# VectorE makes every seventh source one-hot only up to quad 66 of 196, ScalarE makes the others

## The chip, the cores and the metric

One core of one Trainium2 chip. The metric is device time in microseconds (us) of one execution of the whole program; the median of several runs is compared. Each execution is one launch with all inputs in HBM.

## The reference, cut to what matters

The program runs four graph layers over one graph of 3125 nodes (64 features) and 100000 edges `src -> dst`. Layers 0, 1 and 3 sum neighbours, `segment_sum(h[src], dst)`, and so need only how often each pair (dst, src) occurs: an adjacency matrix of counts. Layer 2 needs each edge for itself, because the message depends on the edge's type:

```python
edge_index = jnp.stack([src, dst])
x = _layernorm(x + _L0_gnn_ref(x, ..., edge_index), axis=-1)      # 2 rounds of segment_sum(h[src], dst)
x = _layernorm(x + _L1_gnn_ref(x, edge_index, ...), axis=-1)      # 1 round
x = _layernorm(x + _L2_gnn_ref(edge_index, edge_type_100, x, ...), axis=-1)  # circular correlation by edge
x = _layernorm(x + _L3_gnn_ref(x, ..., src, dst), axis=-1)        # 1 round
```

The edges come sorted by `dst`. The change lies in the stage that builds the adjacency matrix, before any layer.

## The kernel before

**The whole.** Up to about 215 us the edges are loaded, keys are computed and ranks for a sort are made. From 215 to 637 us the adjacency matrix is counted (the stage of the change). Then layers 0 and 1 run as dense products with that matrix (to about 1110 us), layer 2 gathers rows by indirect DMAs that GpSimd issues (line 1615, in two rounds, to about 3200 us), and layer 3 is again a dense product.

**The counting stage.** The edges are cut into 196 quads (`NQ`) of 4 x 128 edges, a quad into 2 pairs of 2 x 128 edges (392 pairs, numbered n; quad q has the pairs 2q and 2q+1). For each 128 edges TensorE multiplies a source one-hot (128 edges x 125, `oh_src`, the weights) with a destination one-hot (128 edges x columns of a window, `oh_dst`), which counts the edges of each (src, dst) into PSUM. Because the edges are sorted, a pair touches a narrow window of nodes. The window is 12 nodes in the first and second quarter of the pairs, 17 in the third and 20 in the fourth; times 25 blocks this makes 300, 300, 425 and 500 columns. The quarters begin at quads 0, 49, 98 and 147. A second small product (line 768) counts degrees with `oh_blk`.

**Who does what.**
- VectorE, for each pair n in order: at every 14th pair `oh_blk` for 7 quads (line 710); if n is even and n // 2 is in `VECTOR_QUADS`, the quad's source one-hot (`make_sources`, line 698: one comparison of 128 x 500); two `oh_dst` (line 720); then `add_unit` (line 691), which adds the PSUM result of the pair 6 back (`PAST`) into the adjacency matrix in SBUF. In the first quarter one such addition serves two pairs. Every 28 pairs it loads 28 window starts into registers (lines 680 and 681).
- ScalarE, for each quad not in `VECTOR_QUADS`: four `Square` activations (line 659, one per 128 edges, into `sq_src`, two buffers) and one `Relu` over all four (line 671), which writes `oh_src`. It makes the squares of its next quad before the Relu of this one.
- TensorE waits for the sources (`src_made` or `src_made_here`, by who made them), for `dst_made`, and for a free PSUM bank, and tells `counted` after every 4th pair (`BATCH`).
- GpSimd issues 392 indirect DMAs, one per column of sorted records (line 295), from 86 us on; it is tied to nothing in this stage.

**What couples them.** `oh_src` has 6 buffers (`SRC_RING`), so a source can be made once the quad 6 earlier has been counted; `oh_dst` has 7 buffers (`DST_RING`), PSUM has 7 banks for the results. At the end of the stage VectorE, ScalarE, TensorE and SyncE join; GpSimd doesn't take part, it only waits for the join before its next part (line 1427).

`VECTOR_QUADS` (line 75) is 3, 10, 17, ... 192: 28 quads. The loop of ScalarE and the one-hot of VectorE:

```python
mine = [q for q in range(NQ) if q not in VECTOR_QUADS]
...
for i, q in enumerate(mine):
    if i + 1 < len(mine):
        if i >= 1:
            act.wait_ge(src_made.sem, i)
        squares(i + 1)
    if q >= SRC_RING:
        act.wait_ge(counted.sem, batches(2 * (q - SRC_RING) + 2))
    act.wait_ge(src_squared.sem, i + 1)
    nc.scalar.activation(oh_src[q % SRC_RING][:], sq_src[i % 2][:], ACT.Relu, ...)
...
if n % 2 == 0 and n // 2 in VECTOR_QUADS:
    make_sources(n // 2)
```

Of the kernel before, what the change touches and what calls it, by code (L numbers as in the profile page):

```python
# [47 lines left out]
NQ = 2 * QUADS  # L48
# [23 lines left out]
BATCH = 4  # L72
QUARTER_PAIRS = PAIRS // 4
WINDOWS = (12, 12, 17, WIN)
VECTOR_QUADS = frozenset(range(3, NQ, 7))
RUNS = 3
CHUNK = 4 * LO
CHUNKS = -(-NODES // CHUNK)
# [88 lines left out]
def gnn_stack(nc, a, out):  # L167
    ctx = ExitStack()
    with ctx:
# [130 lines left out]
        with sort:  # L300
# [44 lines left out]
            with together() as block:  # L345
                @block.vector
                def _(dve):
                    link = Chain(dve, vec)
                    for t, v in ((src_i, -1), (dst_i, -1), (typ_i, 0), (nat_src_i, -1), (nat_dst_i, -1)):
                        link(nc.vector.memset(t[:], v))  # L350
                    link(nc.vector.memset(empty[:], 0))
                    link(nc.vector.memset(rank[:], float(RUN * 200)))
                    link(nc.vector.memset(ones_f[:], 1.0))
                    link.close()
# [282 lines left out]
        with ExitStack() as t2:  # L637
# [13 lines left out]
            with together() as block:  # L651
                @block.scalar
                def _(act):
                    mine = [q for q in range(NQ) if q not in VECTOR_QUADS]

# [19 lines left out]
                def _(dve):  # L675
# [18 lines left out]
                    def make_sources(q):  # L694

                        if q >= SRC_RING:
                            dve.wait_ge(counted.sem, batches(2 * (q - SRC_RING) + 2))
                        v.tensor_tensor(oh_src[q % SRC_RING][:],
                                        iota[:, 0:LO].rearrange("p (a l) -> p a l", a=1).to_broadcast([P, QUAD, LO]),
                                        nat_lo[:, q * QUAD:(q + 1) * QUAD].rearrange("p (t a) -> p t a", a=1).to_broadcast([P, QUAD, LO]),  # L700
                                        ALU.is_equal).then_inc(src_made_here.sem, 1)

                    units_added = 0
                    for n in range(PAIRS + 1):
                        if n < PAIRS:
                            if n % (2 * STEP) == 0:
                                u = n // (2 * STEP)
                                if u >= 2:
# [5 lines left out]
                                    .to_broadcast([P, STEP * QUAD, BLOCKS]), ALU.is_equal).then_inc(blk_made.sem, 1)  # L714
                            if n % 2 == 0 and n // 2 in VECTOR_QUADS:
                                make_sources(n // 2)
# [28 lines left out]
                def _(pe):  # L745
                    nc.tensor.matmul(psum[0:LO, deg_bank:deg_bank + BUCKETS], zeros[:], zeros[:, 0:BUCKETS],
                                     start=True, stop=False, skip_group_check=True)
                    for n in range(PAIRS):
# [4 lines left out]
                        if n % 2 == 0:  # L753
                            if q in VECTOR_QUADS:
                                pe.wait_ge(src_made_here.sem, sum(k <= q for k in VECTOR_QUADS))
                            else:
                                pe.wait_ge(src_made.sem, sum(k not in VECTOR_QUADS for k in range(q + 1)))
                        unit = UNIT_OF[n]
# [1766 lines left out]
```

## Time and profile before

| | us |
|---|---|
| median of 3 runs | 3346.01 |
| the runs | 3328.13, 3346.01, 3346.45 |
| time of the profiled execution | 3341.13 |
| its span in the profile | 3339.3 |
| counting stage in it | about 215 to 637 |

A busy time is the time in which an engine ran instructions; a wait is put down to what ended it. "Granted clock" is TensorE's clock as a share of full speed. PE is TensorE, PEld its weight loads, DVE VectorE, ACT ScalarE, POOL GpSimd. The page of the profile gives sums over the whole span; the views by stretches, by tile, of waits and of instructions in order of time cut out the counting stage.

### The profile page before, as it was taken

What the parts mean: (1) busy time and instruction counts of PE and PEld (TensorE: products, weight loads), DVE (VectorE), ACT (ScalarE), POOL (GpSimd) and SP (SyncE); (2) the same over time, 40 slices, a digit from 0 to 9 for tenths busy, and PEclk for the clock granted to TensorE, in tenths of its full rate; (3) what the DMA queues carried; (4) which work ended last, traced back from release to release, by engine and by line L of the source; (5) the groups of instructions that cost most, each with busy time, mean ns of one, the idle gap of its engine ahead of it and who ended that gap; (6) DMA issues with size and microseconds to landing.
All of it is one profiled execution on the core that took longest, in us unless ns stands there. A gap on an engine that the chain in (4) does not pass through costs nothing.

```text
span 3339.3 us, 43437 instructions
## 1 busy us (share of the span) xinstructions
PE 2045.3 (61%) x12631; PEld 1588.5 (48%) x12632; DVE 1638.4 (49%) x4094; ACT 1324.1 (40%) x3259; POOL 1987.7 (60%) x2031
## 2 busy tenths in 40 slices
PE   0038878656748586555655555656666666666657
PEld 0027644323324375555655555535555555555544
DVE  7939999744453432222222222345444454444452
ACT  4249876200121074433534334244334353334322
POOL 0777777202212377777777777277777777777700
PEclk9555565667768655555555555578777787777778
DMA  1000000073400132222222222153222323223271
GB/s 37 1 1 2 2 2 2 7 130 62 56 4 2 46 77 55 52 54 52 53 53 53 54 52 49 43 134 84 78 78 79 79 78 78 79 77 78 61 169 38
DMA packets 172646, 183.05 MB, mean 55 GB/s; under 512 B 68506, under 2 KB 145414, under 8 KB 171667
## 3 DMA queue, kind: packets, MB, share of 16 engines
q1 hardware_dynamic: 100801, 99.30, 13.7%
q0 software_dynamic: 64960, 78.47, 9.5%
q10 hardware_dynamic: 6656, 2.40, 0.3%
q8 instruction: 122, 2.00, 0.2%
q14 instruction: 107, 0.88, 0.1%
HBM read 153.41 MB, written 26.60 MB: 54 GB/s over the span
## 4 chain that ended last, share of the span: by engine, by line
POOL 40%; issue 17%; DVE 16%; PE 15%; DMA 5%; ACT 3%; DVEq 1%; SPq 1%; PEldq 0%; ACTq 0%; PEld 0%; POOLq 0%
POOL adj_again_middle L1615 37%; PE psum L1168 4%; DVE adj L691 4%; DVE oh_dst L720 3%; POOL sorted_edges L295 3%; DMA adj_again_middle<-gather_table,gidx_s 3%; PE psum L1735 2%; PE psum L1164 2%; DVE adj_again_middle L1687 2%; DMA sorted_edges<-block_rows,run_rows 2%; ACT sq_src L659 1%; PE psum L1771 1%; PE psum L1406 1%; ACT oh_src L671 1%; DMA l_v<-in_L_gnn_beta 1%
## 5 line engine op out<-in xcount | busy, mean ns | idle before, releaser
L1615 POOL DMA_INDIRECT adj_again_middle<-gather_table,gidx_s x1568 | 1505.4, 960 | 555.3 <-issue 468.4
L1687 DVE TENSOR_TENSOR adj_again_middle<-adj_again_middle,psum 128x256 f32<-128x256 f32 x1176 | 442.1, 417 | 1141.5 <-DMA adj_again_middle<-gather_table,gidx_s 830.6
L1735 PE MATMUL psum<-rel_parts,oh_t 128*128 128x96 bf16 (+1 forms) x4704 | 564.9, 288 | 709.9 <-DVE adj_again_middle L1687 558.5
L1655 ACT ACTIVATE adj_again_middle<-cst,lo_s 128x125 f32<-128x125 f32 x1664 | 527.1, 388 | 1071.8 <-PE psum L1771 1068.2
L1735 PEld LDWEIGHTS psum<-rel_parts,oh_t 128*128 128x128 bf16 x4704 | 415.8, 127 | 828.6 <-issue 581.2
L1771 PE MATMUL psum<-adj_again_middle,oh_s 128*125 x3328 | 739.0, 381 | 23.7 <-issue 16.7
L1771 PEld LDWEIGHTS psum<-adj_again_middle,oh_s 128*125 128x125 f32 x3328 | 662.5, 288 | 48.8 <-issue 42.6
L295 POOL DMA_INDIRECT sorted_edges<-rec,row_i x392 | 393.2, 1003 | 213.2 <-issue 127.1
L766 PE MATMUL psum<-oh_dst,oh_src 128*125 128x300 bf16 (+2 forms) x784 | 337.3, 522 | 73.0 <-DVE oh_dst L720 55.2
L1427 POOL DMA_INDIRECT sorted_edges<-block_rows,run_rows x64 | 86.7, 1355 | 377.9 <-ACT block_rows L1416 266.5
L1659 ACT ACTIVATE oh_s<-adj_again_middle,cst 128x500 f32<-128x500 f32 x416 | 296.1, 712 | 13.6
L766 PEld LDWEIGHTS psum<-oh_dst,oh_src 128*125 128x125 bf16 x784 | 154.9, 198 | 181.0 <-issue 77.2
L659 ACT ACTIVATE sq_src<-cst,x 128x125 bf16<-128x125 f32 x672 | 212.8, 389 | 61.7 <-SPq L221 56.3
L720 DVE TENSOR_SCALAR oh_dst<-iota,x 128x300 bf16<-128x300 int16 (+2 forms) x784 | 219.7, 326 | 2.1 <-PE psum L768 2.1
L1711 DVE TENSOR_TENSOR adj_again_middle<-adj_again_middle 128x256 f32<-128x256 f32 (+1 forms) x392 | 217.2, 554 | 6.8
L1168 PE MATMUL psum<-adj,parts 125*128 125x500 bf16 (+1 forms) x525 | 153.1, 443 | 79.1 <-DVEq L221 79.1
L691 DVE TENSOR_TENSOR adj<-adj,psum 125x300 f32 (+2 forms) x343 | 188.4, 549 | 22.0 <-issue 20.5
L768 PE MATMUL psum<-oh_blk,oh_src 128*125 128x25 bf16 x784 | 172.6, 220 | 0.0
L768 PEld LDWEIGHTS psum<-oh_blk,oh_src 128*125 128x125 bf16 x784 | 169.3, 216 | 0.0
L1679 DVE TENSOR_SCALAR oh_t<-tb,cst 128x512 bf16<-128x512 bf16 x392 | 148.1, 378 | 6.3 <-DMA tb<-sorted_types 6.2
L671 ACT ACTIVATE oh_src<-sq_src,cst 128x500 bf16<-128x500 bf16 x168 | 117.6, 701 | 76.9 <-PE psum L768 76.7
L1168 PEld LDWEIGHTS psum<-adj,parts 125*128 125x128 bf16 x525 | 56.2, 123 | 134.2 <-issue 114.3
(408 smaller groups left out, 1388.8 us busy)
## 6 DMA issues: line engine op xcount, KB each, us to landing
tb<-sorted_types SPq DMA_DIRECT2D x392, 128.0 KB, 3.2
adj_again_middle<-gather_table,gidx_s POOLq DMA_INDIRECT x1568, 2.5
adj_saved<-adj SPq DMA_DIRECT2D x6, 2734.4 KB
adj_again_middle<-adj_saved SPq DMA_DIRECT2D x3, 2734.4 KB
sorted_edges<-rec,row_i POOLq DMA_INDIRECT x392
adj_again_last<-adj_saved SPq DMA_DIRECT2D x2, 2734.4 KB
adj_again_first<-adj_saved SPq DMA_DIRECT2D x1, 2734.4 KB
adj_saved<-adj SPq DMA_DIRECT2D x6, 317.4 KB
```

Of the source, the lines that this page charges most:

```text
L295: nc.gpsimd.indirect_dma_start(rec_d[0], bass.IndirectOffsetOnAxis(ap=row_i[:, c:c + 1], axis=0), rec[:, c, :], None).then_inc(sent.sem, 16)
L691: v.tensor_tensor(to, to, psum[0:LO, pair_bank(u):pair_bank(u) + wide_ * BLOCKS].rearrange("p (n s) -> p s n", s=BLOCKS), ALU.add).then_in ...
L720: ins = v.tensor_scalar(oh_dst[n % DST_RING][:, k, 0:pair_window(n) * BLOCKS], iota16[:, 0:pair_window(n) * BLOCKS], nat_key[:, 2 * n + k: ...
L766: nc.tensor.matmul(psum[0:LO, pair_bank(unit):pair_bank(unit) + wc], of, oh_dst[n % DST_RING][:, k, 0:wc], start=(begins and k == 0), stop ...
L768: mm = nc.tensor.matmul(psum[0:LO, deg_bank + h * BLOCKS:deg_bank + (h + 1) * BLOCKS], of, oh_blk[n // (2 * STEP) % 2][:, n % (2 * STEP) * ...
L1168: nc.tensor.matmul(psum[:, to:to + w], parts12[:, s, :], adj(s, c), start=(s == 0), stop=False, skip_group_check=True)
L1615: nc.gpsimd.indirect_dma_start(gx[g % DEEP][:, k, :], None, table_d[d], bass.IndirectOffsetOnAxis(ap=gidx_s[:, t:t + 1], axis=0),).then_in ...
L1655: sq = nc.scalar.activation(sq_s[:, k, :], iota[:, 0:LO], ACT.Square, bias=lo_s[:, t:t + 1], scale=-1.0)
L1659: nc.scalar.activation(oh_s[g % OH_S][:], sq_s[:], ACT.Relu, bias=one_col, scale=-2.0).then_inc(oh_s_made.sem, 1)
L1687: mul = v.tensor_tensor(part_prod[:, u * SUB:(u + 1) * SUB, s, :].rearrange("p g (a f) -> p g a f", a=2), rows[:, :, s * d // 2:(s + 1) * ...
L1735: mm = nc.tensor.matmul(ps_rel[:, k * RS:k * RS + W], oh_t[g % (AHEAD + 1)][:, (u * SUB + k) * P:(u * SUB + k + 1) * P], rel_parts[:, s, : ...
L1771: mm = nc.tensor.matmul(psum[0:LO, bass.ds((buckets[n] - less) * d, d)], oh_s[j % OH_S][:, k, :], prod[:, bass.ds(tiles[n] * d, d)], start ...
```

## The change

`VECTOR_QUADS` keeps its first 10 members (3, 10, ... 66) and loses the 18 from 73 on (73, 80, ... 192). For those 18 quads VectorE's comparison is gone, and ScalarE makes four squares and a Relu for each. The semaphore counts that TensorE waits for follow from the set. Nothing else changes.

```diff
-VECTOR_QUADS = frozenset(range(3, NQ, 7))
+VECTOR_QUADS = frozenset(range(3, 70, 7))
```

## Rows read from the trace of the kernel before

**Rows 1.** The page: span, and busy time of each engine over it.
```profile
span 3339.3 us, 43437 instructions
PE 2045.3 (61%) x12631; PEld 1588.5 (48%) x12632; DVE 1638.4 (49%) x4094; ACT 1324.1 (40%) x3259; POOL 1987.7 (60%) x2031
```

**Rows 2.** Stretches of the counting stage: busy time (instructions) by engine, clock, DMA.
```profile
215.00:340.40 125.40, 103.91 (x582) 88.10 (x583) 112.28 (x404) 123.29 (x332) 94.06 (x95) 0.57 0.02 2
340.40:389.20 48.80, 41.24 (x206) 31.56 (x204) 46.01 (x159) 42.24 (x112) 35.13 (x37) 0.50 0.02 2
389.20:501.60 112.40, 89.09 (x392) 55.84 (x392) 107.72 (x309) 83.06 (x215) 86.32 (x86) 0.63 0.02 2
501.60:607.00 105.40, 90.39 (x317) 48.16 (x318) 103.11 (x252) 65.33 (x169) 78.49 (x80) 0.53 0.02 1
607.00:628.50 21.50, 15.87 (x75) 8.83 (x74) 21.50 (x57) 5.60 (x14) 0.49 (x1) 0.78 0.01 1
```

**Rows 3.** Waits from 340.4 to 628.5 us: total, times, longest.
```profile
ACT oh_src L671 <- PE psum L768: 76.7, 47, 3.5
...
PE psum L766 <- DVE oh_dst L720: 46.2, 68, 1.9
...
PEld psum L766 <- DVE oh_src L698: 16.2, 18, 1.2
DVE adj L691 <- issue: 9.6, 9, 1.4
```

**Rows 4.** Stretches, line 698 on DVE alone.
```profile
340.40:628.50 288.10, 12.01 (x18) 0.58 0.02 2
```

**Rows 5.** DVE in order of time around quad 73: start, duration, what.
```profile
340.51 0.67 DVE L698 TENSOR_TENSOR oh_src<-cst,x 128x500 bf16<-128x500 f32 x1
341.10 0.50 DVE L720 TENSOR_SCALAR oh_dst<-iota,x 128x300 bf16<-128x300 int16 x2
```

**Rows 6.** ACT in order of time, just before quad 73.
```profile
335.04 0.70 ACT L671 ACTIVATE oh_src<-sq_src,cst 128x500 bf16<-128x500 bf16 x1
...
336.94 0.70 ACT L671 ACTIVATE oh_src<-sq_src,cst 128x500 bf16<-128x500 bf16 x1
```

**Rows 7.** Stretches, line 671 on ACT alone.
```profile
215.00:336.00 121.00, 43.85 (x63) 0.57 0.02 2
```

**Rows 8.** Stretches, line 720 on DVE alone.
```profile
215.00:338.90 123.90, 69.88 (x288) 0.57 0.02 2
...
340.40:389.20 48.80, 25.70 (x100) 0.50 0.02 2
389.20:501.60 112.40, 57.07 (x196) 0.63 0.02 2
501.60:607.00 105.40, 55.18 (x160) 0.53 0.02 1
607.00:628.50 21.50, 10.87 (x36) 0.78 0.01 1
```

**Rows 9.** DVE in order of time, two pairs while GpSimd works, fourth quarter.
```profile
551.75 0.75 DVE L720 TENSOR_SCALAR oh_dst<-iota,x 128x500 bf16<-128x500 int16 x2
...
553.01 0.76 DVE L720 TENSOR_SCALAR oh_dst<-iota,x 128x500 bf16<-128x500 int16 x2
```

**Rows 10.** POOL in order of time, the same stretch.
```profile
551.20 0.96 POOL L295 DMA_INDIRECT sorted_edges<-rec,row_i  x1 [0.31 <-issue]
552.46 0.96 POOL L295 DMA_INDIRECT sorted_edges<-rec,row_i  x1 [0.30 <-issue]
```

**Rows 11.** DVE in order of time around quad 178 (source one-hot at 582.60).
```profile
582.60 0.67 DVE L698 TENSOR_TENSOR oh_src<-cst,x 128x500 bf16<-128x500 f32 x1
583.19 0.59 DVE L720 TENSOR_SCALAR oh_dst<-iota,x 128x500 bf16<-128x500 int16 x2
...
584.29 0.59 DVE L720 TENSOR_SCALAR oh_dst<-iota,x 128x500 bf16<-128x500 int16 x2
```

**Rows 12.** Stretch of layers 0 and 1: busy time by engine, clock, DMA.
```profile
700.00:1110.00 410.00, 282.26 (x1898) 159.96 (x1897) 181.69 (x362) 56.12 (x133) 88.34 (x66) 0.75 0.31 50
```

## The prediction

> **What bounds the kernel now.** I read the page first, for the span and the shares [rows 1]: no engine is busy for more than 61% of the span, so the kernel is a row of stages with different limits, and a busy share of the whole says nothing about an edit to one of them. The stage of this edit is the counting stage, and there I read the view by stretches, cut where the order of the work changes: at quad 73, the first that changes hands (340.4 us), and at the starts of the third and fourth quarter (389.2 and 501.6) [rows 2]. Up to quad 73 ScalarE is busy 123.3 of 125.4 us: it bounds. From quad 73 on it has slack that grows (42.2 of 48.8, then 83.1 of 112.4, then 65.3 of 105.4 us), and VectorE is full: 46.0 of 48.8, 107.7 of 112.4, 103.1 of 105.4, 21.5 of 21.5 us. Together that is 278.3 of 288.1 us. The idle rest is 9.8 us, and the view of waits has 9.6 us of it in 9 pauses at line 691, ended by "issue": these are the loads of window starts into registers, VectorE's own work [rows 3]. The same view shows who follows whom: ScalarE waits 76.7 us for TensorE to give buffers back, TensorE waits 46.2 us for destination one-hots of VectorE and 16.2 us more for its source one-hots. So after quad 73 the end of the stage is VectorE's end, and the change takes work from the engine that sets it and gives it to one with slack. Before quad 73, where ScalarE bounds, nothing changes.
>
> **What goes from VectorE.** 18 comparisons at line 698, all between 340.4 and 628.5 us, 12.0 us busy by themselves [rows 4]. Their price on the path is less than their duration, because one instruction starts before the other ends: the comparison of quad 73 starts at 340.51 and the next instruction at 341.10, so it costs 0.59 us [rows 5]; the one of quad 178, at 582.60 and 583.19, costs the same 0.59 [rows 11]. 18 x 0.59 = 10.6 us.
>
> **What ScalarE gets.** Four squares and a Relu per quad, and it has a period of its own for them: two Relus follow each other at 335.04 and 336.94, 1.90 us [rows 6]. For 18 quads that is 34.2 us on an engine that waits 76.7 us in the same stretch [rows 3]. But slack in sum isn't enough, it must be there quad by quad:
> - At the handover. By 336.0 us ScalarE has started 63 Relus [rows 7], which are quads 0 to 72 without VectorE's ten; its next Relu, at 336.94, will be that of quad 73. VectorE has started 288 destination one-hots, four for each of quads 0 to 71, by 338.9 [rows 8], and would begin those of quad 73 at 340.5. ScalarE starts with a lead of 3.6 us.
> - In the rest of the second quarter. VectorE takes 48.8 us for 25 quads (100 one-hots [rows 8]); without its four comparisons 48.8 - 2.4 = 46.4 us, 1.86 us a quad, against 1.90 for ScalarE. ScalarE loses 25 x 0.04 = about 1 us of the 3.6. The Relu lasts 0.70 us and TensorE needs its result only when the first pair of one-hots (0.50 us [rows 5]) is there, so some 2 us are left. This is the narrowest place, and I cost it at nothing. If the lead were gone, the 25 quads would take 25 x 1.90 = 47.5 us instead of 46.4: 1.1 us lost of the 2.4 won there.
> - Later. The third quarter has 49 quads in 112.4 us, 108.3 without its seven comparisons, 2.21 us a quad; the fourth (126.9 us up to 628.5) comes to 2.5. ScalarE needs 1.90: covered.
>
> The other resources: TensorE is busy 90.4 of 105.4 us in the fourth quarter at a granted clock of 0.53 [rows 2]; with six comparisons less (3.5 us) that is 90.4 of 101.9, still 11% free. Its 16.2 us of waits for VectorE's sources go too, but they were no part of VectorE's time. A source can be made once the quad 6 earlier is counted; that holds ScalarE back now and will again, quads ahead of need. No DMA and no wait of SP or POOL is moved.
>
> **What the shorter VectorE gives back.** One term is not free. In the fourth quarter two destination one-hots take 0.75 us while GpSimd issues its DMAs, and the pairs follow each other at 551.75 and 553.01, every 1.26 us [rows 9]; GpSimd's DMAs start at 551.20 and 552.46, every 1.26 us too [rows 10]. Right behind a comparison the same two take 0.59 and the pairs follow at 583.19 and 584.29, every 1.10 us [rows 11]. So VectorE, whose pair needs 1.10, is held to GpSimd's beat when it has caught up with it, 0.16 us a pair, and a comparison in between puts it 0.59 us behind the beat, which buys it 0.59 / 0.16, some four pairs at full speed. In sum a one-hot costs 55.18 / 160 = 0.345 us up to 607 and 10.87 / 36 = 0.302 after GpSimd has ended [rows 8]: 160 x 0.043 = 6.9 us of stretch in this quarter. Taking away the six comparisons before 607 therefore gives back between 0 and 6 x 0.59 = 3.5 us. Three of the six (157, 171, 185) stand right ahead of a register load, which puts VectorE 1.1 us behind the beat anyway (9.6 / 9 [rows 3]), so I take a third, 1.1 us. In the second and third quarter the pair doesn't match the beat and I take nothing.
>
> The Trainium skill has a rule on this ("SBUF — State Buffer", Who interferes with whom): VectorE in its two-port modes, which `tensor_scalar` can enter, and GpSimd hold a shared port pair exclusively, and the loser "fully blocks" for the whole instruction of the other. The trace agrees that they collide but shows a loss of 0.16 us, not one of up to 0.96. By the rule VectorE would go by GpSimd's beat in all of the fourth quarter and the gain there would be gone; that is the second case below, priced from rows.
>
> **The sum.** 10.6 - 1.1 = 9.5 us off the stage. What follows (the joined start of the next part, the dense layers, GpSimd's gathers from about 1190 us) begins at the join and moves earlier as a whole: GpSimd is busy for 0.49 us after 607 and then done [rows 2], the join is at about 637. The profiled execution took 3341.1, so it would take 3331.6. The median of the runs lies 4.9 us above it; against that, 3346.0 - 9.5 = 3336.5. The three runs spread over 18 us, twice the gain, so I say 3336 us.
>
> **Rivals.**
> 1. *GpSimd's beat absorbs the fourth quarter.* Then the six comparisons bring nothing, and 12 x 0.59 = 7.1 us remain: 3339. For it: rows 9 and 10 show the lock. Against: 80 pairs at 1.26 are 100.8 us, the stretch lasts 105.4 [rows 2], so it isn't paced by GpSimd throughout.
> 2. *Nothing arrives at the end.* The gain of the stage is eaten later, by GpSimd's DMAs of the gathers meeting other work differently, or ScalarE bounds after all. 3346, within 3 us. Against: no work after the join is tied to a clock of its own.
> 3. *Slower: the one-hots collide with GpSimd more often.* Place: the 196 one-hots of the third quarter and those of the fourth; price 0.16 us a pair. Locked pairs now are about 6.9 / 0.16 = 43 of 80. If all 49 x 2 = 98 pairs of the third quarter came to be held (15.7 us) and the 37 others of the fourth (5.9 us), the change would cost 21.6 - 10.6 = 11 us: 3357. It decides from 10.6 / 0.16 = 66 more held pairs on. Against: a third-quarter pair needs some 1 us and would have to be held 0.26 for the beat, more than the 0.16 seen, so it slips through.
> 4. *TensorE's clock falls out otherwise.* From 700 to 1110 us TensorE is busy 282 us at a mean granted clock of 0.75 [rows 12], a mixture of both levels, 1.2 and 2.4 GHz. A busy us per matmul is 90.39 / 317 = 0.285 at a clock of 0.53 and 15.87 / 75 = 0.212 at 0.78 [rows 2], a third more for 0.25 of clock. If the stretch fell to the lower level throughout, that would be up to 282 x 0.34 = 96 us more, of which the waited-for part counts, 3346 + 96 = 3442 at the worst; if it rose, some tens less. Nothing ties either to this edit.
>
> **How the numbers follow.** Chances: forecast 0.60 (3331 to 3340 on the median), rival 1 0.15, rival 2 0.12, rival 3 0.07, rival 4 0.06, equally on both sides. All but the last lie within the 1% (33 us) that a measurement of this kernel can tell from no change. So faster by over 1% 0.03, within 1% 0.94, slower 0.03. The range must also hold the spread of the runs, 3328 to 3346 before, 9.5 us less: 3318 to 3337 for the forecast, and up to 3346 + 6 for rivals 2 and 3: 3317 to 3352. The forecast's sign is "faster by 0.3%", most likely too small to be told.
>
> **What the profile after would show.** Line 698 ten times, line 671 186 times. ScalarE's Relu of quad 73 at 336.9 and Relus every 1.90 us up to the end of the second quarter; if instead TensorE waits there for ScalarE's line 671 by more than 2 us, the lead was too thin. 492 one-hots begin at 340.5 and the last six additions end near 624 instead of 634. Line 720's mean between the fourth quarter's start and 607 rises from 0.345, by up to 0.02 us, if the beat takes back its share. The start of the gathers is earlier by the same 9 to 10 us. I would be wrong if the stage gets shorter by less than 6 us or longer, or if it does and the end doesn't follow.

## The result, and the profile after

| us | before | after |
|---|---|---|
| median of 20 runs | 3335.89 | 3329.85 |
| the runs | 3328.13 to 3346.45 | 3324.63 to 3336.21 |
| span of the profiled execution | 3339.3 | 3329.2 |
| counting stage in it, first destination one-hot to last addition | 417.5 | 412.7 |

The ratio is 0.9979, 95% interval 0.997 to 0.9989: 0.2% faster, 3.7 to 10 us. (With more runs the median before came to 3335.9 instead of the 3346.0 of the first three.) A second comparison later, 12 runs against 23, gave 0.9979 again, interval 0.9967 to 0.9992.

The page of the kernel after, to be read against [rows 1]:

```profile
span 3329.2 us, 43527 instructions
...
PE 2033.2 (61%) x12631; PEld 1581.7 (48%) x12632; DVE 1628.5 (49%) x4076; ACT 1356.0 (41%) x3349; POOL 1985.6 (60%) x2031
```

VectorE has 18 instructions less and ScalarE 90 more (18 x 5), 31.9 us more busy. The waits in the counting stage after quad 73 (340.4 to 619 us) answer to [rows 3]; columns are total, times, longest:

```profile
PE psum L766 <- DVE oh_dst L720: 49.7, 73, 2.3
ACT oh_src L671 <- PE psum L768: 40.2, 32, 2.4
...
DVE adj L691 <- issue: 14.2, 9, 2.0
PEld psum L766 <- ACT oh_src L671: 5.3, 14, 0.8
PE psum L766 <- ACT oh_src L671: 3.1, 3, 1.2
```

ScalarE's slack fell from 76.7 to 40.2 us, and VectorE is still not kept waiting by it. But one line is not as it was: the nine pauses at line 691 sum to 14.2 us, where they had 9.6. Nothing in the change touches them. The stage's length can be read from the first and last starts of two VectorE lines (durations are min/median/max in ns), before:

```profile
L720 DVE TENSOR_SCALAR oh_dst<-iota,x x784: 169/323/574, 215.7 to 627.7; 128x300 bf16<-128x300 int16 x98, 128x425 bf16<-128x425 int16 x49, 128x500 bf16<-128x500 int16 x49
L691 DVE TENSOR_TENSOR adj<-adj,psum x343: 400/582/681, 224.6 to 633.2; 125x300 f32 x74, 125x425 f32 x49, 125x500 f32 x49
```

and after:

```profile
L720 DVE TENSOR_SCALAR oh_dst<-iota,x x784: 168/322/540, 216.2 to 623.4; 128x300 bf16<-128x300 int16 x98, 128x425 bf16<-128x425 int16 x49, 128x500 bf16<-128x500 int16 x49
L691 DVE TENSOR_TENSOR adj<-adj,psum x343: 400/581/680, 225.1 to 628.9; 125x300 f32 x74, 125x425 f32 x49, 125x500 f32 x49
```

633.2 - 215.7 = 417.5 and 628.9 - 216.2 = 412.7: the stage is 4.8 us shorter, not 9.5. (Stages here and below are taken from the unrounded starts of the traces, so they can differ by 0.1 us from a subtraction of the rounded ones.) How exact is that? The first quarter of the edges, where the change does nothing, took 81.6 us before and 82.0 after, so such a difference is good to about half a us.

### The profile page after: what moved, and what is told of

The parts are those of the page before. It is cut to its first block, busy times and chain, and to the rows that moved or that the text cites. A ratio compares the mean times of both kernels' runs of the same rounds, so it can differ in the third digit from the quotient of the medians.

```text
span 3329.2 us, 43527 instructions
## 1 busy us (share of the span) xinstructions
PE 2033.2 (61%) x12631; PEld 1581.7 (48%) x12632; DVE 1628.5 (49%) x4076; ACT 1356.0 (41%) x3349; POOL 1985.6 (60%) x2031
## 4 chain that ended last, share of the span: by engine, by line
POOL 43%; issue 17%; DVE 14%; PE 13%; ACT 5%; DMA 4%; DVEq 1%; SPq 0%; PEldq 0%; PEld 0%; ACTq 0%; POOLq 0%
POOL adj_again_middle L1615 40%; PE psum L1168 4%; DVE adj L691 3%; POOL sorted_edges L295 3%; ACT sq_src L659 3%; DVE oh_dst L720 2%; PE psum L1164 2%; DMA adj_again_middle<-gather_table,gidx_s 2%; ACT oh_src L671 2%; PE psum L1735 2%; DVE adj_again_middle L1687 1%; DMA sorted_edges<-block_rows,run_rows 1%; PE psum L1406 1%; DVE block_ones L1392 1%; DMA l_v<-in_L_gnn_beta 1%
## 5 line engine op out<-in xcount | busy, mean ns | idle before, releaser
L1615 POOL DMA_INDIRECT adj_again_middle<-gather_table,gidx_s x1568 | 1508.4, 962 | 553.0 <-issue 470.5
L766 PE MATMUL psum<-oh_dst,oh_src 128*125 128x300 bf16 (+2 forms) x784 | 325.3, 506 | 80.4 <-DVE oh_dst L720 60.4
L659 ACT ACTIVATE sq_src<-cst,x 128x125 bf16<-128x125 f32 x744 | 235.7, 389 | 62.3 <-SPq L221 56.3
L671 ACT ACTIVATE oh_src<-sq_src,cst 128x500 bf16<-128x500 bf16 x186 | 129.9, 699 | 40.3 <-PE psum L768 40.2
```

The costliest lines, as they stand in the source:

```text
L659: sq = nc.scalar.activation(sq_src[i % 2][:, k, :], iota[:, 0:LO], ACT.Square, bias=nat_lo[:, q * QUAD + k:q * QUAD + k + 1], scale=-1.0)
L766: nc.tensor.matmul(psum[0:LO, pair_bank(unit):pair_bank(unit) + wc], of, oh_dst[n % DST_RING][:, k, 0:wc], start=(begins and k == 0), stop ...
L1615: nc.gpsimd.indirect_dma_start(gx[g % DEEP][:, k, :], None, table_d[d], bass.IndirectOffsetOnAxis(ap=gidx_s[:, t:t + 1], axis=0),).then_in ...
```

## Where the other half went: a load that the comparison had hidden

The pauses at line 691 stand where VectorE's sequencer loads 28 window starts from SBUF into registers (line 680). The view of that line in the kernel before:

```profile
L680 DVEq TENSOR_LOAD <-base_u x14: 1847/1852/2102, 221.4 to 599.8; - x14
```

The load keeps the sequencer (the part of the engine that hands instructions over) for 1.85 us, and register operations of line 681 follow it before the addition can be handed over. The view of the chain of work that ended last shows them at quad 157 in the kernel before (start, us of the chain, what; DVEq is VectorE's sequencer):

```profile
525.14 0.34 DVEq L680
...
527.28 0.23 DVEq L681
...
527.54 0.18 DVEq L681
...
527.94 0.68 DVE adj L691
```

From the start of the load to the start of the addition it is 527.94 - 525.14 = 2.80 us. What has been handed to the engine before the load runs on in that time; after that the engine stands still. At quad 157 this looks so before (DVE in order of time; in brackets the idle time ahead):

```profile
525.40 0.66 DVE L691 TENSOR_TENSOR adj<-adj,psum 125x500 f32 x1
525.99 0.66 DVE L698 TENSOR_TENSOR oh_src<-cst,x 128x500 bf16<-128x500 f32 x1
526.57 0.60 DVE L720 TENSOR_SCALAR oh_dst<-iota,x 128x500 bf16<-128x500 int16 x2
527.94 0.68 DVE L691 TENSOR_TENSOR adj<-adj,psum 125x500 f32 x1 [0.77 <-issue]
```

and after:

```profile
522.09 0.66 DVE L691 TENSOR_TENSOR adj<-adj,psum 125x500 f32 x1
522.67 0.76 DVE L720 TENSOR_SCALAR oh_dst<-iota,x 128x500 bf16<-128x500 int16 x2
524.59 0.68 DVE L691 TENSOR_TENSOR adj<-adj,psum 125x500 f32 x1 [1.16 <-issue]
```

From addition to addition it is 2.54 us before and 2.50 after, although a comparison of 0.59 us is gone (the pause grew by 0.39 us, and the two one-hots took 0.76 instead of 0.60). The comparison ran in the shadow of the load. Loads come at every 28th pair, 6 pairs late, which is at quads 73, 87, ... 185, and `VECTOR_QUADS` has every one of these: nine of the eighteen comparisons taken away stood in such a shadow. The pauses grew by (14.2 - 9.6) / 9 = 0.51 us each, so a comparison there is worth under 0.1 us, and the sum becomes about 9 x 0.59 + 9 x 0.06 = 5.9 us. The change's load at this place shows the same 2.80 us (it starts at 521.79, the addition at 524.59): the sequencer's part has one length, and the pause is what the queued work leaves of it. This was an explanation after the fact, so it was put to the test.

## The experiments

**Each half of the comparisons by itself.** Two kernels that differ from the one before only in the set:

```diff
-VECTOR_QUADS = frozenset(range(3, NQ, 7))
+VECTOR_QUADS = frozenset([*range(3, 70, 7), *range(73, NQ, 14)])   # keep_at_load
+VECTOR_QUADS = frozenset([*range(3, 70, 7), *range(80, NQ, 14)])   # keep_between
```

> VectorE keeps, of the 18 comparisons that the change takes from it, the nine at quads 73, 87, ... 185, which stand right ahead of a load of window starts into registers; the nine between them (80, 94, ... 192) go to ScalarE. The stage is measured from VectorE's first destination one-hot to its last addition: 417.5 us before, 412.7 us with the whole change. Cover theory (a comparison ahead of a load hides 0.53 of its 0.59 us in the 1.85 us that the load takes on VectorE's sequencer): the nine kept cost 9 x 0.06 = 0.5 us against the whole change, so 413.2 us, and the nine pauses at line 691 from 340 us on sum to about 9.6 us as before, not to the 14.2 us of the whole change. Rival, all comparisons are worth the same and GpSimd's beat takes half of it back: halfway, 415.1 us.

> The other half: VectorE keeps the nine comparisons at quads 80, 94, ... 192, which stand between two loads, and the nine right ahead of a load (73, 87, ... 185) go to ScalarE. Cover theory: removing these brings 9 x 0.06 = 0.5 us, so the stage stays at about 417.0 us of 417.5, and the pauses at line 691 from 340 us on grow to about 14.2 us. Rival, all comparisons alike: halfway, 415.1 us, with pauses of about 12 us or no rule in them.

Line 691 and the pauses of keep_at_load (its line 720 starts at 215.6):

```profile
L691 DVE TENSOR_TENSOR adj<-adj,psum x343: 400/584/680, 224.6 to 628.8; 125x300 f32 x74, 125x425 f32 x49, 125x500 f32 x49
```

```profile
DVE adj L691 <- issue: 9.6, 9, 1.4
```

and of keep_between (its line 720 starts at 215.9):

```profile
L691 DVE TENSOR_TENSOR adj<-adj,psum x343: 400/585/680, 224.9 to 632.5; 125x300 f32 x74, 125x425 f32 x49, 125x500 f32 x49
```

```profile
DVE adj L691 <- issue: 14.2, 9, 2.0
```

Stages of 413.2 and 416.5 us. So the nine comparisons between loads, which keep_at_load gives away, are worth 417.5 - 413.2 = 4.3 us (0.48 each) and the nine ahead of a load 1.0 us (0.11 each); together they make up what the change brought, within half a us. The pauses came out as expected to the tenth. "All comparisons are alike" (415.1 for both) falls. These kernels ran once each, with 3332.3 and 3338.1 us against 3334.1 for the kernel before beside them; single runs spread too widely to add to this.

**GpSimd out of the way.** The prediction had put the give-back down to GpSimd's beat. To see what that takes, GpSimd's record DMAs were moved behind the stage (its issues and the transfers that they start together, so the two aren't told apart):

```diff
-        send_records(FIRST_SENT, HC)
...
+        counted_through = joins[0]
+
+        @running[0].gpsimd
+        def _(pool):
+            pool.wait_ge(joined.sem, counted_through)
+        send_records(FIRST_SENT, HC)
```

> The kernel before with GpSimd's last 296 record DMAs held back until the counting stage has joined, so that GpSimd does nothing in it; all is computed, but the whole takes hundreds of us longer, and only the counting stage is read. Port theory (a destination one-hot that meets GpSimd's DMA issue is held up to 0.17 us): the stretched one-hots go, 27 + 8 + 50 of them after 293 us with 12 us in sum, so the stage takes about 405 us, and the fourth quarter's pairs follow each other every 1.10 us throughout. Rival, the stretch has another cause: 417 us and pairs at 1.26 us remain.

> The whole change with GpSimd's last 296 record DMAs held back in the same way. Against the quiet kernel before: cover theory, 9 x 0.59 + 9 x 0.06 = 5.9 us less, about 399 us. Rival, GpSimd's beat is what takes back the missing half of the gain: without it the full 18 x 0.59 = 10.6 us appear, about 394.5 us. The part that the beat takes is the difference of this gain to the 4.8 us seen with GpSimd at work: 1 us by the cover theory, 6 us by the rival.

The destination one-hots and additions of quiet_before (lines moved up by one):

```profile
L719 DVE TENSOR_SCALAR oh_dst<-iota,x x784: 285/319/352, 215.9 to 618.2; 128x300 bf16<-128x300 int16 x98, 128x425 bf16<-128x425 int16 x49, 128x500 bf16<-128x500 int16 x49
```

```profile
L690 DVE TENSOR_TENSOR adj<-adj,psum x343: 453/591/680, 224.8 to 623.7; 125x300 f32 x74, 125x425 f32 x49, 125x500 f32 x49
```

and of quiet_after:

```profile
L719 DVE TENSOR_SCALAR oh_dst<-iota,x x784: 283/316/352, 215.7 to 612.5; 128x300 bf16<-128x300 int16 x98, 128x425 bf16<-128x425 int16 x49, 128x500 bf16<-128x500 int16 x49
```

```profile
L690 DVE TENSOR_TENSOR adj<-adj,psum x343: 451/591/680, 224.7 to 618.1; 125x300 f32 x74, 125x425 f32 x49, 125x500 f32 x49
```

No one-hot takes longer than 0.352 us now (0.574 before), and the pairs of the fourth quarter follow at 545.10, 546.20, 547.31 (1.10 us). Of the 97 intervals between the pairs of that quarter 29 were near 1.26 us (1.22 to 1.30) before, 45 with the change, and 1 in either quiet kernel. The stages are 407.8 and 402.4 us, so GpSimd's DMAs cost VectorE 9.7 us in this stage before and 10.3 after. The port theory was right in kind; its 12 us were 2 too many. But the gain of the change without GpSimd is 5.5 us, against 4.8 with it: the beat takes 0.7 us, a difference hardly larger than the half us to which stages agree. In the fourth quarter alone, from first to last destination one-hot, the change won 1.6 us with GpSimd (from 126.0) and 2.5 without it (from 119.0), so there the beat took 0.9. Either way it isn't where the other 5 of the 10.6 us went. The 5.5 agree with the 5.9 of the shadow.

**The load itself out of the way.** If the load is the cause, it must be possible to hide it. The window starts were loaded 14 at a time into two register sets in turn, at every 14th pair, behind the long degree one-hot and ahead of need:

```diff
-AT_ONCE = 28
+AT_ONCE = 14
...
-                        dve.load(regs, base_u[0:1, first:first + AT_ONCE])
+                        dve.load(regs[s], base_u[0:1, first:first + AT_ONCE])
...
+                            if n % AT_ONCE == 0:
+                                load_bases(n)
```

> The kernel before with the window starts loaded 14 at a time into two sets of registers in turn, at every 14th pair, right behind the degree one-hot (0.80 us) and six pairs ahead of their first use; VectorE keeps all 28 comparisons. Cover theory (the load occupies VectorE's sequencer for 1.85 us, and only what the sequencer had queued ahead of it runs on): queued are now an addition 0.58, the degree one-hot 0.80 and two destination one-hots 0.52, in sum 1.9 us, so the pauses at line 691 nearly vanish though there are twice as many loads: from 340 us on 9.6 us become 2 at most, and the stage goes from 417.5 to about 410 us. Rival (the pause comes from the number of loads or from the registers' use in the addition, wherever the load stands): pauses stay at 10 us or double, the stage is 417 us or longer.

> The whole change together with the early loads. Cover theory: comparisons no longer hide a load, so each of the 18 is worth its full 0.59 us where VectorE bounds. In the third and fourth quarter (14 comparisons) the stage loses 14 x 0.59 = 8.3 us against the kernel before with early loads, less 1 us for GpSimd's beat. In the second quarter VectorE would need only some 1.7 us a quad and ScalarE needs 1.90, so ScalarE bounds there and the four comparisons bring nothing: stage about 410 - 7 = 403 us, and TensorE waits for ScalarE's line 671 in the second quarter. Rival, comparisons bring half as with late loads: 405.5 us or more, no waits for ScalarE.

> Early loads, and the comparisons placed where ScalarE bounds: VectorE makes quads 0, 5, ... 45, then 58, 68, ... 98, none later. First quarter: VectorE needs 1.45 + 0.2 x 0.59 = 1.57 us a quad and ScalarE 0.8 x 1.90 = 1.52, against 81.6 / 49 = 1.66 now; second quarter 1.70 + 0.06 = 1.76 against 1.87; third 2.1 against 2.29; fourth about 2.5 against 2.6. Sum of the four: some 20 to 27 us less than 417.5, so a stage of 391 to 397 us and a total 0.6 to 0.8% below the kernel before. Rival, TensorE (1.41 us a quad at the lower clock in the first two quarters) becomes the bound once VectorE and ScalarE are near it: stage 405 us or more, with VectorE waiting at line 691 or 720 for TensorE.

> The changed kernel as it is, once more, for comparison on the same chip: 0.2% below the kernel before, stage 412.7 us within 0.5 us.

This failed. The stages were 426.1, 418.0 and 414.8 us (412.6 for the change as it is, which repeated); early_load took 3357.9 us and early_load_after 3343.2 in their one run, early_load_best had ratio 0.9994 (0.9981 to 1.0006). What came as expected is the difference: between early_load and early_load_after the comparisons are worth 8.1 us (7 were expected, 4.5 by the rival), though both stages are long. The first quarter of early_load_best did take 76 us as forecast, so it wasn't TensorE that bounded: VectorE paused 19.5 us at the additions and 5.3 us at the one-hots, ended by "issue". The loads of early_load, and one of them in order of time on DVE:

```profile
L682 DVEq TENSOR_LOAD <-base_u x28: 1315/2372/3195, 215.3 to 618.0; - x28
```

```profile
472.92 0.58 DVE L693 TENSOR_TENSOR adj<-adj,psum 125x425 f32 x1
473.43 0.87 DVE L712 TENSOR_TENSOR oh_blk<-cst,nat_blk 128x700 bf16<-128x700 f32 x1
474.23 0.56 DVE L722 TENSOR_SCALAR oh_dst<-iota,x 128x425 bf16<-128x425 int16 x2
476.64 0.60 DVE L693 TENSOR_TENSOR adj<-adj,psum 125x425 f32 x1 [1.86 <-issue]
```

In order of time the loads alternate: 1.32, 3.18, 1.32, 3.18 us. Those of 1.32 left no pause or at most 0.3 us (0.8 at the first of all). Those of 3.18 left 1.6 to 2.1 us, 1.86 here: this load starts at 472.85 and the addition at 476.64, 3.79 us later (the load and 0.6 us of register operations and handing over), against 1.9 us of queued work. Every second load differs from the others in two ways: it goes to the second register set, and it begins at an odd multiple of 56 bytes. The next kernels kept the two sets and changed the load alone, by starting each load at a multiple of 16 bytes and reading 16 words:

```diff
-                        dve.load(regs[s], base_u[0:1, first:first + AT_ONCE])
+                        s, skip = first // AT_ONCE % 2, first % 4
+                        dve.load(regs[s], base_u[0:1, first - skip:first - skip + AT_ONCE + 2])
```

> As early_load (window starts for 14 pairs, two register sets, loaded at every 14th pair right behind the degree one-hot; all 28 comparisons kept), but each load begins at a multiple of four words of the tile and reads 16 words. In early_load the loads of 14 registers took 1.32 us when they began at byte 0 of 112 and 3.18 us when they began at byte 56. If the start address makes that difference: all 28 loads take about 1.4 us, the 1.9 us of work queued ahead hides them, pauses at line 691's addition and at the destination one-hots are under 3 us in the whole stage (27.2 in early_load), and the stage is about 405 us (before 417.5, early_load 426.1). Rival, the second register set makes it slow: every second load stays at 3.2 us and the stage at about 426 us.

> The whole change with the aligned early loads. Cover theory: the comparisons hide nothing any more, so against aligned_load each of the 14 in the third and fourth quarter brings its 0.59 us, less 1 to 2 us for GpSimd's beat, and the four of the second quarter bring little, because ScalarE's 1.90 us a quad bounds there: 6 to 8 us less, a stage of 397 to 399 us. Rival, comparisons bring half whatever the loads do: 4.8 us less.

> Aligned early loads with VectorE making quads 0, 5, ... 45 and 58, 68, ... 98 only. First quarter 76.0 us as in early_load_best, second 86, third 103, fourth 123, tail 5: a stage of about 393 us, 24 us or 0.7% less than before (early_load_best had 414.8 us). Rival, TensorE at its lower clock bounds once VectorE's pauses are gone: 400 us or more.

Loads and additions of aligned_load:

```profile
L682 DVEq TENSOR_LOAD <-base_u x28: 1096/1100/1360, 215.0 to 597.7; - x28
```

```profile
L693 DVE TENSOR_TENSOR adj<-adj,psum x343: 400/577/679, 221.9 to 620.5; 125x300 f32 x74, 125x425 f32 x49, 125x500 f32 x49
```

The loads take 1.10 us (the first 1.36), the pauses put down to "issue" are all but gone (0.8 us in two, 27.2 in early_load), and the stage is 404.7 us (from 215.7), 12.8 less than before. So the second register set doesn't make a load slow. Whether the start address alone does it isn't shown: this load also reads 16 words and not 14, so it is address, count or both. With the loads hidden the change still isn't worth 10.6 us: aligned_load_after has a stage of 398.2 us, 6.5 less, within what was expected, but not by the parts expected. (Both ran once, 3327.3 and 3321.3 us.) The stretches from quad 73 to the third quarter, the third quarter, and the fourth up to the last one-hots, line 722 (`oh_dst`) on DVE alone, in aligned_load:

```profile
340.10:386.00 45.90, 25.83 (x101) 0.50 0.02 2
386.00:491.90 105.90, 54.77 (x197) 0.63 0.02 2
491.90:613.50 121.60, 64.50 (x192) 0.59 0.02 2
```

and in aligned_load_after:

```profile
339.70:383.80 44.10, 25.43 (x100) 0.50 0.02 2
383.80:486.10 102.30, 55.84 (x196) 0.73 0.02 2
486.10:607.00 120.90, 68.07 (x192) 0.63 0.02 2
```

With the 0.6 us of quad 73's own comparison, which falls just ahead of the first stretch, the second quarter won 2.4 us of 4 x 0.59, the third 3.6 of 7 x 0.59, and the fourth only 0.7 of 7 x 0.59 = 4.1. There the mean of a one-hot rose from 64.50 / 192 = 0.336 to 68.07 / 192 = 0.355 us, 3.6 us in sum: here GpSimd's beat does take nearly everything, as the prediction's first rival had it. 57 of the quarter's 97 intervals between pairs are near 1.26 us, against 27 in aligned_load. The reading is that neither comparisons nor register pauses put VectorE behind the beat any more; no run tests it by itself. ScalarE did not bound in the second quarter, against the expectation: TensorE waited for it more often in the whole stage, but VectorE hardly longer for TensorE (10.6 us against 9.9 in aligned_load), so its lead was used up and no more. It had nothing to spare, though: in the third quarter it was busy 100.5 of 102.3 us. TensorE's waits for ScalarE in the whole stage of aligned_load_after:

```profile
PEld psum L768 <- ACT oh_src L671: 34.8, 60, 1.2
PE psum L768 <- ACT oh_src L671: 25.4, 42, 2.8
```

(19.4 and 16.8 us in aligned_load). Putting VectorE's comparisons where ScalarE bounds gives the best kernel: aligned_load_best has a stage of 392.2 us and a median of 3310.8 us (3309.9 to 3316.5) against 3337.6 beside it, ratio 0.9925, interval 0.9906 to 0.9944. That is 25 us off the whole, as much as the stage lost, and clear of both kernels of this case. TensorE, the rival there, did not become the bound. The stage came out as forecast, but its parts only in sum: the first quarter took 74.0 us (76 forecast), the second 89.0 (86).

## Why the prediction was right, and where its sum was not

The stated range, 3317 to 3352 us, held the measured 3329.85, and the forecast of a small gain (0.3% forecast, 0.2% measured) was right. But part of that is luck. The 3336 us were reckoned from a median of three runs, 3346.0; from the 3335.9 of twenty the same 9.5 us would have given 3326.4. The narrower forecast of 3331 to 3340 missed for that reason, and the wide range hid it. The gain of the stage, 4.8 us, is half the 9.5 of the sum, and by the prediction's own last sentence (wrong if the stage gets shorter by less than 6 us) the sum failed. By its steps:

- *VectorE sets the end after quad 73.* Right: the stage got shorter by VectorE's part alone, and the gain is there at the end. The last matmuls of the kernel (line 2490) start at 3308.1 instead of 3317.9. Of these 9.8 us 4.3 were there at the end of the stage (it also began 0.5 later). The rest is spread: in the eleven profiles with GpSimd at work the same code took 470.5 to 477.7 us from the last addition to the first matmul of line 1862 (476.6 before, 474.0 with the change) and 2225.7 to 2236.0 from there to the end (2229.5, 2226.3). The medians differ by 6.0, with 4.8 inside the interval.
- *18 x 0.59 = 10.6 us.* This is the term that was mis-sized. 0.59 is the price of a comparison between two instructions that the sequencer hands over without delay; it was read at quad 73 and 178 from the next start [rows 5, 11]. Quad 73 is itself one of those ahead of a load, but the start of the next instruction can't show it: the pause comes after that, at the addition. Nine of the eighteen stood ahead of a register load, where the engine would have stood still anyway. They measured 0.1 us each (keep_between), the other nine 0.48 (keep_at_load), and the whole sum 5.5 (quiet kernels). The sign was in reach: the prediction named the nine pauses as the register loads and counted them as VectorE's own fixed work [rows 3], and even noted that a comparison stands right ahead of them. It did not ask what the pause would be without it. The views of lines 680 and 681, some 2.8 us of the sequencer's own from load to addition against 1.07 us of pause, would have said that 1.7 us at each load was covered by queued work, the comparison among it.
- *ScalarE has slack quad by quad.* Right, and with little to spare in the second quarter as said: TensorE waited 0.8 us for ScalarE in what was left of the second quarter (the prediction would have called the lead too thin from 2 us on). From quad 73 to the end of the stage these waits grew from 3.9 to 8.4 us without reaching VectorE. In aligned_load_after, where VectorE is faster, the lead was used up, still at no cost that shows.
- *GpSimd's beat gives back 1.1 us.* Right in size: 0.7 us by the whole stage of the quiet kernels, 0.9 by their fourth quarter. The fourth quarter's mean for a one-hot did rise, from 0.345 to 58.62 / 167 = 0.351 us, up to 607:

```profile
499.00:607.00 108.00, 58.62 (x167) 0.63 0.02 1
```

- *The rival that GpSimd paces the fourth quarter* did not come here, but it is real: it came in aligned_load_after. The Trainium skill ("SBUF — State Buffer", Who interferes with whom) says that VectorE in a two-port mode and GpSimd share a pair of ports exclusively, the loser blocked for the other's whole instruction. The quiet kernels agree that the two engines collide (9.7 us over 784 one-hots), but not on the price: the longest one-hot took 0.574 us with GpSimd at work and 0.352 without, 0.22 more, and an issue lasts 0.96. No run shows in which mode the one-hots ran.
- *Rivals 2, 3 and 4* did not come. The mean granted clock from 700 to 1110 us was 0.75 before and after.

## What to carry to other kernels

Price an instruction that you remove by what starts later without it, at each kind of place where it stands, and not by one clean place: ahead of a pause its work may be free. Ask of every pause called "issue" what the sequencer does in it and how much engine work was queued ahead; here a register load was hidden by moving it behind the longest instruction and ahead of need, but only once it was also short (early_load was slower, aligned_load faster), and after that the balance between engines had to be found again. Read a price on the path at the next point where the engine may stand still, not at the next start. A pattern of period 7 laid over one of period 14 meets it every second time, so look at where a change falls in the other patterns of the loop.

## What the runs showed of the hardware

- A load of SBUF words into VectorE's registers keeps its sequencer for 1.85 us with 28 words, 1.10 us with 16 words and 1.32 us with 14 words, all from an address that is a multiple of 16 bytes, and for 3.18 us with 14 words from an odd multiple of 56 bytes (the first load of a run takes 0.25 us more). That 16 words are quicker than 14 was not expected; whether the count or the start matters most was not separated further. Register operations and the handing over add 0.95 us behind a load of 28 and 0.6 behind one of 14 before the next addition starts (quad 157 before, 472.85 us in early_load).
- VectorE's one-hot comparison (int16 in, bf16 out, `tensor_scalar`) took at most some 0.2 us longer beside GpSimd's indirect DMAs (an issue lasts 0.96 us). But where a loop of 1.10 us ran beside one of 1.26 us, it was held again and again and took on the other's period: 29 of 97 intervals in the fourth quarter before, 57 of 97 in aligned_load_after.
